# First attention: value matmuls of 512 columns, one column group per unit and head, the two halves of a block's sums added by DVE

## The reference, cut to what matters

```python
scores = jnp.einsum('bqhd,bkhd->bhqk', q, k) * scale
lag = jnp.abs(idx[:, None] - idx[None, :]).astype(jnp.float32)
scores = scores * jnp.exp(-alpha * lag * DT)
attn = jax.nn.softmax(scores, axis=-1)
out = jnp.einsum('bhqk,bkhd->bqhd', attn, v).reshape(B, T, D)
return out @ Wo.T + bo
```

## Time and profile before

| | us |
|---|---|
| median of 3 runs | 3439.34 (3436.93 to 3444.93) |
| the profiled execution | 3449.83 |
| its span | 3448.1 |
| value matmuls L839, first to last start | 292.6 to 1786.9 |
| PE / DVE / ACT / POOL busy over the span | 3081.9 / 2430.8 / 1803.2 / 1421.1 |

### The profile page before, as it was taken

One profiled execution on the slowest core, in us unless ns is written; L12 is line 12 of the kernel. 1 busy time (PEld: TensorE's weight loads), 2 busy tenths in 40 slices (PEclk: granted clock), 3 DMA queues, 4 the chain that ended last, 5 costly groups with the idle time before them and its releaser, 6 DMA issues. The chain is left out here.

```text
span 3448.1 us, 65998 instructions
## 1 busy us (share of the span) xinstructions
PE 3081.9 (89%) x22948; PEld 1745.0 (51%) x22949; DVE 2430.8 (70%) x6509; ACT 1803.2 (52%) x2255; POOL 1421.1 (41%) x741
## 2 busy tenths in 40 slices
PE   3678999999999999999966999869999987999997
PEld 1232333333333333333324556546666666999995
DVE  4679999999999999999747788734555554333334
ACT  4235888888888888888863333322222222111112
POOL 6346787787877877878600000000000111111110
PEclk8788999999999999999987999979989988999998
DMA  5575433333334444334121110030000005555555
GB/s 153 144 191 134 92 84 83 83 80 78 76 69 91 92 92 89 85 82 86 38 49 34 25 25 1 1 115 14 14 14 14 20 21 177 183 182 182 183 183 180
DMA packets 201698, 304.65 MB, mean 88 GB/s; under 512 B 86192, under 2 KB 150544, under 8 KB 199248
## 3 DMA queue, kind: packets, MB, share of 16 engines
q1 hardware_dynamic: 192640, 277.89, 31.3%
q0 software_dynamic: 7632, 22.16, 1.8%
q10 hardware_dynamic: 1152, 1.05, 0.1%
HBM read 238.91 MB, written 62.13 MB: 87 GB/s over the span
## 5 line engine op out<-in xcount | busy, mean ns | idle before, releaser
L870 DVE CUSTOM_DVE_ANT_0 ps_r<-ps_r,toep 128x512 f32<-128x512 f32 x1894 | 1252.4, 716 | 70.9 <-PE ps_r L799 30.8
L969 ACT ACTIVATE prob<-ps_s,csc 128x1024 f32<-128x1024 f32 x768 | 829.9, 1118 | 151.3 <-PE ps_s L823 129.6
L927 POOL TENSOR_TENSOR tb<-tb,toep 128x1024 f32<-128x1024 f32 x240 | 568.1, 2367 | 263.6 <-ACT tb L959 241.1
L799 PE MATMUL ps_r<-p 96*128 96x512 bf16 x1894 | 646.3, 382 | 9.4 <-DVE mp L870 4.1
L823 PE MATMUL ps_s<-p 120*128 120x512 bf16 (+1 forms) x2048 | 609.2, 380 | 26.9 <-ACT tb L959 16.4
L930 POOL TENSOR_TENSOR tb<-tb,mb 128x1024 f32<-128x1024 f32 x240 | 567.8, 2366 | 18.8
L839 PE MATMUL ps_o<-prob,vp 128*32 128x256 f32 x8192 | 548.2, 385 | 1.2 <-ACT prob L966 0.9
L799 PEld LDWEIGHTS ps_r<-p 96*128 96x128 bf16 x1894 | 181.4, 96 | 405.5 <-DVE mp L870 257.9
L839 PEld LDWEIGHTS ps_o<-prob,vp 128*32 128x32 f32 x8192 | 213.7, 109 | 269.6 <-issue 177.9
L823 PEld LDWEIGHTS ps_s<-p 120*128 120x128 bf16 (+1 forms) x2048 | 189.6, 98 | 237.1 <-ACT tb L959 46.6
L2327 ACT ACTIVATE e_aT<-e_u 128x1024 f32<-128x1024 f32 x71 | 75.0, 1057 | 424.3 <-DVE e_u L2398 424.3
(11 more groups left out here) (324 smaller groups left out, 3585.7 us busy)
## 6 DMA issues: line engine op xcount, KB each, us to landing
moe_w<-in_W_dram SPq DMA_DIRECT2D x79, 1024.0 KB, 11.8
p<-scr_scratch SPq DMA_DIRECT2D x288, 192.0 KB
mb<-mrow_scratch SPq DMA_DIRECT2D x16, 2048.0 KB, 8.1
scr_scratch<-part SPq DMA_DIRECT2D x64, 384.0 KB, 6.9
p<-scr_scratch SPq DMA_DIRECT2D x96, 128.0 KB
moe_pt<-slots_scratch SPq DMA_DIRECT2D x72, 132.0 KB, 2.1
vscr_scratch<-vsb SPq DMA_DIRECT2D x8, 1024.0 KB, 9.1
vp<-vscr_scratch SPq DMA_DIRECT2D x16, 512.0 KB, 22.2
```

The lines of the kernel that those rows point to most:

```text
L799: pe.matmul(ps_r[:, bank, :], buf[:, hh, 0, qt * P:(qt + 1) * P], buf[:, hh, 1, kc * CH:(kc + 1) * CH], start=True, stop=True)\
L870: dve.tensor_tensor_reduce(ps_r[:, bank, :], ps_r[:, bank, :], toep[:, col:col + CH], 1.0, -3.0e38, ALU.mult, ALU.max, mp[:, whose.par, hh ...
L927: pool.tensor_tensor(tb[:, k % DIAGS], tb[:, k % DIAGS], toep[:, col:col + CH].unsqueeze(1) .broadcast_to([P, 2, CH]), ALU.mult).then_inc( ...
L969: act.activation(prob[:, n % RING], ps_s[:, mine % 2], ACT.Exp, scale=csc[:, qb * TB + kb:qb * TB + kb + 1]).then_inc(s["exp"], 1)
```

## The change

A batch of value matmuls is now four instructions of 512 columns: each of the two units takes two column groups, one per head, so the two units run into different partitions and are not added up by the accumulation. `ps_o` is one result of 128 x 512. ACT evacuates 512 columns, PE transposes four pieces, and DVE adds the two units' halves (numerators and sums alike) before it divides. The ring's bank is released after DVE's second instruction of four. `rec` counts four steps a block.

```diff
-        ot = ctx.enter_context(nc.sbuf_tensor("ot", [P, WIDE], F32))
-        rec = ctx.enter_context(nc.sbuf_tensor("rec", [P, 2, 4], F32))
+        ot = ctx.enter_context(nc.sbuf_tensor("ot", [P, CH], F32))
+        both = ctx.enter_context(nc.sbuf_tensor("both", [P, TPC, 2, HD + 1], F32))
+        rec = ctx.enter_context(nc.sbuf_tensor("rec", [P, TPC, 2], F32))
-        ps_o = ctx.enter_context(nc.psum_tensor("ps_o", [P, 2, WIDE], F32))
+        ps_o = ctx.enter_context(nc.psum_tensor("ps_o", [P, CH], F32))
...
-                        hold(sp, s["ring_free"], first_slot(this) + slot_of(kind, "sum", QB - 1, ahead) + 1, s["passed"])
+                        hold(sp, s["rec"], 4 * (j.times(QB) + QB), s["passed"])
...
-                                for f in range(2):
-                                    for hh in range(2):
-                                        q = 2 * f + hh
-                                        out = ps_o[32 * q:32 * q + VW, qb % 2, :]
-                                        mm = pe.matmul(out.rearrange("p (j c) -> p j c", c=P), vp[whose.par][:, kb, hh, :],
-                                                       prob[:, m % RING, hh, :].rearrange("p (j f c) -> p f j c", f=2, c=P)[:, f],
-                                                       start=(m % TB == 0), stop=(m % TB == TB - 1), skip_group_check=True)
+                                for hh in range(2):
+                                    q = 2 * (m - n) + hh
+                                    mm = pe.matmul(ps_o[32 * q:32 * q + VW, :], vp[whose.par][:, kb, hh, :], prob[:, m % RING, hh, :],
+                                                   start=(n % TB == 0), stop=(n % TB == TB - 2), skip_group_check=True)
                                 mm.then_inc(s["value"], 1)
...
-                            for j in range(2):
+                            for j in range(TPC):
                                 mm = pe.transpose(ps_r[:, bank, j * P:(j + 1) * P], ot[:, j * P:(j + 1) * P], ident[:])
...
-                            got = ps_r[:, bank, 0:WIDE].rearrange("p (j q d) -> p j q d", j=2, d=VW)
+                            got = ps_r[:, bank, :].rearrange("p (j u h d) -> p u j h d", u=2, h=2, d=VW)
+                            done = 4 * (whose.times(QB) + n)
                             dve.wait_ge(s["ring_free"], up_to(at_slot))
-                            dve.reciprocal(rec[:].unsqueeze(3), got[:, :, :, HD:HD + 1]).then_inc(s["rec"], 1)
-                            dve.wait_ge(s["rec"], up_to(whose.times(QB) + n + 1))
-                            dve.tensor_tensor(at[:, whose.par, n * TPC:(n + 1) * TPC, :].rearrange("p (j f) (h d) -> p j (f h) d", f=2, h=2),
-                                              got[:, :, :, 0:HD], rec[:].unsqueeze(3).broadcast_to([P, 2, 4, HD]),
-                                              ALU.mult).then_inc(s["ring_free"], 1)
+                            dve.wait_ge(s["rec"], up_to(done))
+                            dve.tensor_copy(both[:], got[:, 0, :, :, 0:HD + 1]).then_inc(s["rec"], 1)
+                            dve.wait_ge(s["rec"], up_to(done + 1))
+                            dve.tensor_tensor(both[:], both[:], got[:, 1, :, :, 0:HD + 1], ALU.add).then_inc(s["ring_free"], 1)
+                            dve.wait_ge(s["ring_free"], up_to(at_slot + 1))
+                            dve.reciprocal(rec[:].unsqueeze(3), both[:, :, :, HD:HD + 1]).then_inc(s["rec"], 2)
+                            dve.wait_ge(s["rec"], up_to(done + 3))
+                            dve.tensor_tensor(at[:, whose.par, n * TPC:(n + 1) * TPC, :].rearrange("p j (h d) -> p j h d", h=2),
+                                              both[:, :, :, 0:HD], rec[:].unsqueeze(3).broadcast_to([P, TPC, 2, HD]),
+                                              ALU.mult).then_inc(s["rec"], 1)
...
-                        act.activation(ot[:], ps_o[:, qb % 2, :], ACT.Copy).then_inc(s["evac"], 1)
+                        act.activation(ot[:], ps_o[:], ACT.Copy).then_inc(s["evac"], 1)
```

## The result

| | before | after |
|---|---|---|
| median, us | 3438.77 (3436.93 to 3444.93, 4 runs) | 3523.41 (3522.14 to 3524.03, 4 runs) |
| ratio, 95% interval | | 1.0232 [1.0208, 1.0256] |
| span of the profiled execution, us | 3448.1 | 3522.3 |
| value matmuls, first to last start, us | 292.6 to 1786.9: 1494.3 | 291.6 to 1872.9: 1581.3 |

The account below looks back on a forecast made before the run. PE's order was taken as the bound, busy 1299 of 1320 us. The terms -3, +12.5, +44.6 and +2.3 sum to +56 us, so 3495 us against the median 3439.3; the range was 3464 to 3530.

Parts of the forecast that it names:

- Bound and path: First attention: PE's order is the path; what PE must do or wait for lengthens the 23.8 us block one for one.
- the two kinds of block: Block sums 1 and 2, without slack: +0.875 us each; sums 0 and 3, where the ring skips a bank: +0.655.
- Value matmuls, -3 us: PE's value batches: two rounds of 512 columns take 0.997 against 1.003 us, over 512 batches -3 us.
- four no longer side by side: Rival, value matmuls: a batch takes three rounds of 0.43 us, +220 us, 3715 us; chance 0.04.
- a long first round: Rival, value matmuls: the batch's first round takes 0.53 us, +44 over the sum, 3539 us; chance 0.05.
- the exposed loads: Rival, value matmuls: weight loads hold up rounds, so two fewer rounds save 112 us against 59 cost, 3386 us; chance 0.04.
- Evacuation, +12.5: ACT's evacuation of 512 columns takes 0.215 us more, on the path to the score matmul, 58 times: +12.5 us.
- Transposes and DVE's sum, +44.6: Each block's sum: two more PE transposes, +0.22 us, and DVE's longer part, +0.655 us, delay PE by 44.6 us overall.
- T4 waits for T1's bank: After a sum's transposes, PE's fourth tile needs the first tile's bank, freed by DVE; it starts at 2.685 us.
- mult 0.29: DVE's final multiply in each sum was priced at 0.29 us, as in the kernel before.
- the surplus stays on DVE: Rival: DVE's extra work does not reach PE, which loses only transposes and evacuation, +18 us, 3457 us; chance 0.10.
- Last pair and end, +2.3: Last pair's sums, 0.3 us by 4, and the unhidden work behind the very last sum before the store: +2.3 us.

Follow-up runs that it names:

- evac_late: Kernel before with ACT's evacuation moved behind the copy of the diagonal unit's scores; ratio to before 0.9952, attention -16.5 us.
- values_alone: Kernel before with only the value matmuls at 512 columns; half the queries and the addition of the units left out; ratio to before 0.9995.
- mult_from_sbuf: Kernel before, but DVE first copies the sums to SBUF and multiplies from there; 3507.11 us, 1.0177 of the kernel before.
- sum_longer: Kernel before with one more DVE instruction per sum, an unused copy of 256 columns from PSUM; ratio to before 1.0042, attention +22.4 us.
- rec_in_psum: Changed kernel with reciprocals written into the ring's PSUM bank, released after the multiply; 3494.56 us, ratio to before 1.0126.

## Why the prediction was right, and where it fell short

- *Bound and path:* right. What was added to PE's order or to what it waits for came out as the chain of the two kinds of block has it. The way back is not one for one: evac_late won 0.29 of 0.41 us a block.
- *Value matmuls, -3 us:* right (batch 5 ns shorter; +1.3 us in the one trace of values_alone). Four run side by side, and the first round takes 0.453 us, not 0.53. The rivals of four no longer side by side and of a long first round are out. So is that of the exposed loads: half of them gone won 5 ns a batch, where it needed 115 for the change to break even.
- *Evacuation, +12.5:* right, +12.6 by itself.
- *Transposes and DVE's sum, +44.6:* this is the step that was mis-sized. That T4 waits for T1's bank is shown by the changed kernel and by mult_from_sbuf, where T4's wait is put down to T1's reading; that DVE's idle time takes nothing up is shown by sum_longer, there over T3. With the contention taken out (rec_in_psum) T4 starts at 2.61 to 2.68 against 2.685 forecast, and the attention is 56.5 longer against a sum of +56. That these agree so well is partly chance, since rec_in_psum holds the bank longer and PE waits at T3. The wrong term is "mult 0.29": I took the duration of a multiply that reads PSUM and one input in SBUF for one with both inputs in SBUF, beside a POOL that is busy 79% of the stretch. It took 0.76, and the gap behind the add 0.12 instead of 0.035, so DVE's part grew by 1.2 us (0.45 to 1.67 in the sums shown, from the sum's first instruction to T1's) and not by 0.655. That is also outside the bound of 0.9 us that the prediction gave it. T4 comes only 0.47 later than forecast, since DVE begins the sum 0.14 us later and not 0.22 (0.55 and 0.69 after the first transpose): two small errors that cancel. 0.47 us for 58 sums is 27 us; the 64 multiplies take 45.8 us in all against 18.6 before, 27 more; the change and rec_in_psum lie 30.5 us apart in the attention and 29 in the medians.
- *Rival "the surplus stays on DVE":* out; every run with more DVE work behind the transposes moved T4.
- *Last pair and end, +2.3:* not measured by itself. POOL rests there, and the last five multiplies take 0.29 us; the one before them, at the seam, took 1.79.
- *Range:* it held by luck. It reached up to 3530 for other causes, a long first round above all, that did not occur; DVE's surplus, which did, had at most +14 us in it and needed 27.
- *Small slips:* by the printed figures a first round of 0.53 costs 0.076 us more a batch, 39 us over the sum and not 44. The times of T4 and of the release of T1's bank differ by 0.06 us in rows 7 and 9, not by 0.01; as T4 follows its release by 0.05 in the changed kernel too, the reading of no slack stands. The line of the earlier trace rows reaches from 350 to 1700 us; from 370 to 1690 there are 55 evacuations, and the period is the same.
- The single edits of the value matmuls, the evacuation and the transposes add up to 23.2 us of attention (1.3 + 12.6 + 9.3). They leave 33.3 of rec_in_psum's 56.5 for DVE's two instructions and the longer hold of the bank; the contention adds 30.5.

Left open: what made the granted clock behind the attention differ between executions.

## What to carry to other kernels

When an operand moves from PSUM to SBUF, the duration of the old instruction is no longer a price: look at what POOL does at that moment, and try to keep one input of a short DVE instruction in PSUM if POOL is busy. Idle time over a stretch is not slack at a place; find the instruction that reuses the buffer and compare its start with the buffer's release, to hundredths of a microsecond. Where an engine's in-order queue waits for one thing while the next instruction's input lies ready, swapping the two can be worth more than the change under study.

## What the runs showed of the hardware

A DVE multiply of 128x128 with both inputs in SBUF did not get done beside POOL's tensor_tensor of 128x1024, which reads SBUF too: in all 118 cases of the two kernels that have it (the change and mult_from_sbuf) it ended 0.14 to 0.16 us after POOL's instruction, whether 0.31 or 2.19 us of that were left. With one input in PSUM the multiply took 0.29 us in the 59 cases of the kernel before and in the 59 of rec_in_psum. Copy from PSUM, add of SBUF and PSUM, and reciprocal of one SBUF input took 0.30, 0.29 to 0.30 and 0.20 us in all 64 sums of the changed kernel, beside POOL or not. In its last pair, where DVE does POOL's work, the multiply from SBUF is short again:

```profile
1826.51 0.29 DVE L910 TENSOR_TENSOR at<-both,rec 128x128 f32<-128x128 f32 x1
```

The Trainium skill (SBUF — State Buffer, SBUF: two separate sides) has this rule: the port pair shared by the two engines is an exclusive lock, taken by a DVE instruction with two SBUF inputs and held by whichever starts first for its whole length. The page gives it for a GpSimd instruction that reads SBUF, as POOL's does here. The runs agree that the multiply is blocked until POOL's instruction ends. An estimate by the rule is 0.29 us and what is left of that instruction, 0.62 at 855.12, so 0.91; 0.77 was seen, because only 0.15 of the 0.29 us stands behind POOL's end. Why it is not all of it no run here shows.

Float32 matmuls of 32 output rows go four side by side in the four column groups, at 256 and at 512 columns alike, at a granted clock of 1.00: the rounds of the batch in the earlier trace rows start at 1002.58, 1002.82 and 1003.04, and at 512 columns a batch has two rounds in 1.0 us, the first 0.453. Of four transposes of 128 columns in a row the second starts 0.165 us after the first, and the fourth 0.384.
